# Keys of an attention kernel reversed in blocks of 128, and 3 of 16 half blocks of bias added by VectorE

## What is computed

```python
bias = tisa_bias(kernel_offsets, kernel_amplitudes, kernel_sharpness, l)   # depends on head and on i - j only
logits = jnp.einsum('bhld,bhmd->bhlm', q, k) * scale + bias[None]
attn = jax.nn.softmax(logits, axis=-1)
out = jnp.einsum('bhlm,bhmd->bhld', attn, v)
```

## Time and profile before

| | |
|---|---|
| median of 3 runs | 952.49 us (952.27 to 953.29) |
| the profiled execution | 943.6 us |
| its span, first to last instruction | 941.9 us |
| PE busy | 824.5 us, 88% |
| DVE busy | 707.9 us, 75% |
| ACT busy | 632.2 us, 67% |
| POOL busy | 244.0 us, 26% |
| granted TensorE clock, mean | 0.948 of full speed |

### The profile page before, as it was taken

How to read it: one execution, slowest core, us unless ns; L and a number is a source line. 1 busy time by engine, 2 the same in 40 slices (tenths; PEclk the granted TensorE clock), 3 DMA queues, 4 the chain that set the end, 5 groups by cost and what they waited for, 6 DMA issues and landing times.

```text
span 941.9 us, 22741 instructions
## 1 busy us (share of the span) xinstructions
PE 824.5 (88%) x9011; PEld 314.7 (33%) x9011; DVE 707.9 (75%) x1105; ACT 632.2 (67%) x1255; POOL 244.0 (26%) x543
## 2 busy tenths in 40 slices
PE   5189999999998999999998999999999999645770
PEld 2023333333333333333332223322232322245670
DVE  5388766777776887667789998899999898056545
ACT  6037767777775677767787988899889899501221
POOL 4010423200000414312300553331004001004773
PEclk9569999999999999999999999999999999866995
DMA  3655534654545454445313343232212220100123
GB/s 91 192 164 172 167 108 154 196 169 149 162 152 176 126 159 160 151 137 165 108 53 102 106 125 98 91 91 74 82 58 63 74 69 30 38 22 27 50 46 97
DMA packets 69439, 104.82 MB, mean 111 GB/s; under 512 B 15814, under 2 KB 45958, under 8 KB 69334
## 3 DMA queue, kind: packets, MB, share of 16 engines
q1 hardware_dynamic: 63254, 68.90, 25.2%
q10 hardware_dynamic: 4608, 31.46, 9.6%
q0 software_dynamic: 1472, 3.02, 1.3%
HBM read 84.23 MB, written 19.01 MB: 110 GB/s over the span
## 4 chain that ended last, share of the span: by engine, by line
PE 66%; DVE 10%; DMA 6%; SPq 5%; POOL 5%; ACT 4%; issue 4%; POOLq 0%; DVEq 0%
PE bank L1205 21%; PE bank L1224 16%; PE bank L1231 14%; PE bank L1185 8%; ACT prob_mem L844 4%; DVE unit_max L936 3%; PE bank L1158 2%; POOL moe_out L749 2%; DVE no_use L933 2%; PE bank L1267 2%; POOL prob_mem L738 2%; DMA prob_mem<-tokens,gather_u 1%; PE bank L1153 1%; DVE stats L882 1%; DMA prob_mem<-unit_sums 1%
## 5 line engine op out<-in xcount | busy, mean ns | idle before, releaser
L844 ACT ACTIVATE prob_mem<-bank 128x512 f32<-128x512 f32 x1024 | 555.8, 597 | 152.2 <-PE bank L1231 129.0
L933 DVE CUSTOM_DVE_ANT_0 no_use<-bank,w_moe 128x1024 bf16<-128x1024 f32 x256 | 311.9, 1223 | 111.4 <-PE bank L1185 110.7
L1185 PE MATMUL bank<-k_rows,q_rows 56*128 56x512 bf16 x1024 | 315.9, 392 | 25.2 <-DMA k_rows<-k_parts 17.3
L1224 PE MATMUL bank<-q_rows,k_rows 59*128 59x512 bf16 x1024 | 322.7, 385 | 4.6 <-DMA q_rows<-maxima_rows 0.9
L1205 PE MATMUL bank<-prob_mem,v_ring 128*32 128x256 f32 x4096 | 319.9, 386 | 6.0 <-issue 5.1
L936 DVE TENSOR_REDUCE unit_max<-bank 128x1 f32<-128x1024 f32 x256 | 297.9, 1216 | 21.5 <-PE bank L1185 19.9
L655 POOL CAST max_parts<-unit_max 128x8 bf16<-128x8 f32 x64 | 12.3, 191 | 574.6 <-DVE unit_max L933 327.4
L1231 PE MATMUL bank<-skew_mem,flip 96*32 96x512 bf16 x2048 | 159.5, 389 | 0.0
L1205 PEld LDWEIGHTS bank<-prob_mem,v_ring 128*32 128x32 f32 x4096 | 103.0, 110 | 159.8 <-ACT prob_mem L844 62.7
L1224 PEld LDWEIGHTS bank<-q_rows,k_rows 59*128 59x128 bf16 x1024 | 80.0, 93 | 218.3 <-issue 111.2
L1185 PEld LDWEIGHTS bank<-k_rows,q_rows 56*128 56x128 bf16 x1024 | 75.9, 93 | 36.0 <-issue 18.5
(11 more groups left out here) (164 smaller groups left out, 514.6 us busy)
## 6 DMA issues: line engine op xcount, KB each, us to landing
w_moe<-bias_rows ACTq DMA_DIRECT2D x32, 960.0 KB, 5.7
q_rows<-q_parts SPq DMA_DIRECT2D x256, 48.0 KB
k_rows<-k_parts SPq DMA_DIRECT2D x128, 96.0 KB
skew_mem<-bias_parts SPq DMA_DIRECT2D x32, 378.0 KB, 3.8
unit_sums<-o_ring SPq DMA_DIRECT2D x64, 128.0 KB, 2.6
w_moe<-in_L_ffn_w_dram SPq DMA_DIRECT2D x16, 256.0 KB, 3.1
q_parts<-prob_mem SPq DMA_DIRECT2D x8, 384.0 KB, 3.1
k_parts<-prob_mem SPq DMA_DIRECT2D x24, 128.0 KB, 2.6
```

The lines of the kernel that those rows point to most:

```text
L844: nc.scalar.activation(prob[:, kb, half * N:(half + 1) * N], b_bank(("exp", exp_no(n, kb, half))), ACT.Exp).then_inc(exp_done, 1)
L933: nc.vector.tensor_tensor_reduce(out=no_use[:, qb % 2, :], in0=scores, in1=bias, scale=1.0, scalar=LEAST, op0=ALU.add, op1=ALU.max, accum_ ...
L1185: return nc.tensor.matmul(sa_slot(QB * m + qb)[:, f, :], q_rows[rows, m % SLOTS, qb * P:(qb + 1) * P], k_rows[rows, m % SLOTS, f * N:(f + ...
L1224: return nc.tensor.matmul(b_bank(("exp", exp_no(n, kb, f))), k_rows[rows, n % SLOTS, kb * P:(kb + 1) * P], q_rows[rows, n % SLOTS, f * N:( ...
```

## The change

Half block `f=0` of blocks 1, 4 and 7 of each stage-1 unit gets its bias from DVE: an in-place addition on the PSUM bank of 512 values from the table, before the `block_max` of that block. PE leaves out the four bias matmuls of these half blocks (96 half blocks in all, 384 matmuls). So that one table serves both, with keys and with queries in the partitions, the keys are reversed within each block of 128; the table is then read forwards, in eight runs of 128, where it was read backwards before. Four tables are held where two were. SP waits for `exp_done` where it waited for `sb_done`.

```diff
+        def by_dve(n, kb, f):
+            return stage_of(n) == 0 and f == 0 and kb in (1, 4, 7)
...
-            queue.dma_start(bias_tab[:, n % 2, :], src).then_inc(tab_loaded[n % 2], 16)
+            queue.dma_start(bias_tab[:, n % 4, :], src).then_inc(tab_loaded[n % 4], 16)
...
+        def reversed_tiles(ap):
+
+            tiles_here = ap.shape[-1] // P
+            return bass.AP(ap.tensor, ap.offset + P - 1, [list(ap.ap[0]), [P, tiles_here], [-1, P]])
...
-                        sp.wait_ge(sb_done, 2 * QB * n)
+                        sp.wait_ge(exp_done, 2 * QB * n)
...
-                        act.wait_ge(sb_done, 2 * (QB * n + kb) + half + 1)
+                        i = exp_no(n, kb, half)
+                        if by_dve(n, kb, half):
+                            act.wait_ge(bias_added, dve_before[i + 1])
+                        else:
+                            act.wait_ge(sb_done, i + 1 - dve_before[i + 1])
...
-                nc.vector.tensor_copy(feat_b[:, gi * N:(gi + 1) * N], bank[:, gi, :]).then_inc(first_feat, 1)
+                nc.vector.tensor_copy(feat_b[:, gi * N:(gi + 1) * N], reversed_tiles(bank[:, gi, :])).then_inc(first_feat, 1)
...
-                    bias = bass.AP(tab.tensor, tab.offset, [list(tab.ap[0]), [-1, L]])
+                    bias = bass.AP(tab.tensor, tab.offset, [list(tab.ap[0]), [-P, QB], [1, P]])
...
+            def add_bias(n, kb):
+
+                half = b_bank(("exp", exp_no(n, kb, 0)))
+                at = L - P - kb * P
+                dve.wait_ge(raw_done, dve_before[exp_no(n, kb, 0) + 1])
+                nc.vector.tensor_tensor(half, half, bias_tab[:, n % 4, at:at + N], ALU.add).then_inc(bias_added, 1)
...
                 for kb in range(QB):
+                    if by_dve(n, kb, 0):
+                        add_bias(n, kb)
                     if n + 2 < NU:
                         block_max(n + 2, kb)
...
-                    nc.tensor.matmul(dst[:, 0:PW], weight, feat_b[:, c * PW:(c + 1) * PW], start=True, stop=True).then_inc(qk_mm, 1)
+                    piece = feat_b[:, c * PW:(c + 1) * PW]
+                    nc.tensor.matmul(dst[:, 0:PW], weight, piece if s else reversed_tiles(piece), start=True, stop=True).then_inc(qk_mm, 1)
...
+                        if by_dve(n, kb, f):
+                            ins.then_inc(raw_done, 1)
...
                         for f in range(2):
-                            bias_b(n, kb, f)
+                            if not by_dve(n, kb, f):
+                                bias_b(n, kb, f)
```

More of the change, by code:

```diff
@@ L91, in sandwich_kernel @@
         w_moe = sb("w_moe", [P, E, 2 * HID])
-        bias_tab = w_moe[:, 0:E // 2, :].rearrange("p e w -> p (e w)")[:, 0:2 * TAW].rearrange("p (s c) -> p s c", s=2)
+        bias_tab = w_moe[:, :, :].rearrange("p e w -> p (e w)")[:, 0:4 * TAW].rearrange("p (s c) -> p s c", s=4)
         skew_mem = sb("skew_mem", [P, 3 * L])
@@ L152, in sandwich_kernel @@
         rstd_twice = sb("rstd_twice", [P, TT])
-        flip = sb("flip", [96, 32], bf16)
+        pick = sb("pick", [96, 32], bf16)
         unit_max = sb("unit_max", [P, 2, QB])
@@ L208, in sandwich_kernel @@
         ones_ready = sem("ones_ready")
-        flip_ready = sem("flip_ready")
+        pick_ready = sem("pick_ready")
         sharp_ready = sem("sharp_ready")
@@ L238, in sandwich_kernel @@
         skew_loaded = [sem(f"skew_loaded{s}") for s in range(3)]
-        tab_loaded = [sem(f"tab_loaded{s}") for s in range(2)]
+        tab_loaded = [sem(f"tab_loaded{s}") for s in range(4)]
         sa_done = sem("sa_done")
@@ L242, in sandwich_kernel @@
         sb_done = sem("sb_done")
+        raw_done = sem("raw_done")
+        bias_added = sem("bias_added")
         exp_done = sem("exp_done")
@@ L366, in sandwich_kernel @@
         b_place = {what: i for i, what in enumerate(b_order)}
+        def by_dve(n, kb, f):
+            return stage_of(n) == 0 and f == 0 and kb in (1, 4, 7)
+        dve_before = [0]
+        for n in range(NU):
+            for kb in range(QB):
+                for f in range(2):
+                    dve_before.append(dve_before[-1] + by_dve(n, kb, f))
         def b_bank(what):
@@ L544, in _ @@
                     if n + LEAD >= SLOTS:
-                        sp.wait_ge(sb_done, 2 * QB * (n + LEAD - SLOTS + 1))
+                        sp.wait_ge(exp_done, 2 * QB * (n + LEAD - SLOTS + 1))
                     rows_of(n + LEAD)
@@ L624, in _ @@
             nc.gpsimd.memset(v_ring[:, :, :, DH:DH + 1], 1.0).then_inc(ones_ready, 1)
-            chain(nc.gpsimd.memset(flip[:], 0.0))
+            chain(nc.gpsimd.memset(pick[:], 0.0))
             for n in range(3):
-                chain(nc.gpsimd.affine_select(out=flip[:], in_=flip[:], compare_op=ALU.not_equal, fill=1.0,
-                                              base=-93 - n, pattern=[[3, 32]], channel_multiplier=1))
-            pool.sem_inc(flip_ready, 1)
+                chain(nc.gpsimd.affine_select(out=pick[:], in_=pick[:], compare_op=ALU.not_equal, fill=1.0,
+                                              base=-n, pattern=[[-3, 32]], channel_multiplier=1))
+            pool.sem_inc(pick_ready, 1)
             pool.wait_ge(bias_out, 1)
@@ L808, in turn_out @@
                 dst, src = feat_b[:, q * PW:(q + 1) * PW], b_bank(("turn", i))[:, 0:PW]
+                if t < 3:
+                    src = reversed_tiles(src)
                 if t in (0, 3):
@@ L929, in block_max @@
                     if qb == 0:
-                        dve.wait_ge(tab_loaded[m % 2], 16 * (m // 2 + 1))
-                    tab = bias_tab[:, m % 2, qb * P + L - 1:qb * P + L]
-                    bias = bass.AP(tab.tensor, tab.offset, [list(tab.ap[0]), [-1, L]])
-                    nc.vector.tensor_tensor_reduce(out=no_use[:, qb % 2, :], in0=scores, in1=bias, scale=1.0, scalar=LEAST, op0=ALU.add,
+                        dve.wait_ge(tab_loaded[m % 4], 16 * (m // 4 + 1))
+                    tab = bias_tab[:, m % 4, qb * P + L - P:qb * P + L - P + 1]
+                    bias = bass.AP(tab.tensor, tab.offset, [list(tab.ap[0]), [-P, QB], [1, P]])
+                    nc.vector.tensor_tensor_reduce(out=no_use[:, qb % 2, :].rearrange("p (k c) -> p k c", k=QB),
+                                                   in0=scores.rearrange("p (k c) -> p k c", k=QB), in1=bias, scale=1.0, scalar=LEAST, op0=ALU.add,
                                                    op1=ALU.max, accum_out=unit_max[:, m % 2, qb:qb + 1]).then_inc(max_done, 1)
@@ L1168, in _ @@
                 pe.wait_ge(first_feat, gi + 1)
-                nc.tensor.matmul(bank[:, 4 + 2 * gi, :], w_in_t[:, 2, :], feat_b[:, cols], start=True, stop=True).then_inc(first_q, 1)
+                nc.tensor.matmul(bank[:, 4 + 2 * gi, :], w_in_t[:, 2, :], reversed_tiles(feat_b[:, cols]), start=True, stop=True).then_inc(first_q, 1)
                 nc.tensor.matmul(bank[:, 5 + 2 * gi, :], w_in_t[:, 0, :], feat_b[:, cols], start=True, stop=True).then_inc(first_k, 1)
@@ L1225, in scores_b @@
                                         q_rows[rows, n % SLOTS, f * N:(f + 1) * N],
-                                        start=True, stop=(stage_of(n) == 1))
+                                        start=True, stop=(stage_of(n) == 1 or by_dve(n, kb, f)))
             def bias_b(n, kb, f):
                 for c in range(4):
-                    at = f * N - kb * P - 32 * c + L - 32
-                    ins = nc.tensor.matmul(b_bank(("exp", exp_no(n, kb, f)))[32 * c:32 * (c + 1), :], flip[:], skew[0:96, n % 3, at:at + N],
+                    at = f * N - kb * P + 32 * c + L - P
+                    ins = nc.tensor.matmul(b_bank(("exp", exp_no(n, kb, f)))[32 * c:32 * (c + 1), :], pick[:], skew[0:96, n % 3, at:at + N],
                                            start=False, stop=True, tile_position=(0, 32 * c))
@@ L1287, in _ @@
                     maxima_t(0, max_t(0))
-            pe.wait_ge(flip_ready, 1)
+            pe.wait_ge(pick_ready, 1)
             for n in range(NU):
```

## The result

The changed kernel takes 961.48 us in the median (958.84 to 963.61), against 952.4 for the kernel before: a ratio of 1.0092 (95% interval 1.0065 to 1.0119), so 8.8 us slower, 6 to 11. The forecast was 959.5, with 949 to 967 for 8 in 10.

What follows compares the result with a forecast made beforehand. PE was taken to bound stage 1. Plain additions 4.3, crowded 2.3 + 0.4, pieces 0.9, minus half a us in unit 0 gave about +7: 952.5 + 7 = 959.5 us, range 949 to 967 for 8 in 10.

Steps and rivals of the forecast that it cites:

- the ring: Reuse of PSUM banks in stage 1: PE's next second pair of score matmuls waits for an exponential; plain-block slack 0.10 us.
- rival A: The 1.81 us from first pair to next second pair holds: +4 to +10 us, 956 to 962.5; chance 0.60.
- the chain of 1.81: First score pair to next second pair, through addition and exponential: 0.43 + 0.69 + 0.03 + 0.60 + 0.06 = 1.81 us, before 1.75.
- D: No change: the 0.06 us loss is too small to read, only crowded blocks cost, 951 to 954 us; chance 0.11.
- PE's part: Bias matmuls PE gives up in stage 1: 96 half blocks of 0.22 us, at most 21 us.
- DVE free in time: In plain stage-1 blocks DVE is free 0.05 us before the addition is due, so the addition does not wait.
- Crowded blocks: Where statistics follow on DVE, additions start 0.25 us late at block 7, 0.57 at block 1: about 2.3 us more.
- Reversing, tables, SP's waits: Backwards reads, the forward-read table, table loads and SP's later waits in stage 1: taken as zero cost.
- Pieces between blocks: 18 additions with a piece behind them: eight at projections gain 0.08 us, ten lose some 0.15; together +0.9 us.
- rival B: The addition is dearer, by writing PSUM or DVE being late more often: 966 us at 0.76, 978 at 0.89; chance 0.16.
- Rival C: The addition hands over to ACT before its row ends, so faster: about 952 us, or 948; chance 0.13.
- the slow clock of unit 0: In unit 0 the slower clock makes bias matmuls dearer, so half a us was subtracted from the sum.

Runs made afterwards that it cites:

- the run with the order alone: The changed kernel with no DVE additions, PE adding all 16 half blocks; reversed keys, forward table and four tables kept: 952.22 us, ratio 0.9985.
- the run with the second half: The changed kernel with DVE adding the bias of half f=1 instead of f=0 at blocks 1, 4 and 7, in place: 946.37 us, ratio 0.9925.

## Why the prediction was right

**The bound and the ring.** The reading that PE bounds stage 1, and that an exponential just 0.10 early keeps the ring from binding, held. Taking the exponential out of the bank's loan, the time from the first pair to the bank's reuse, turned the loss into a gain with DVE's work unchanged. So rival A, the chain of 1.81, is what happened (961.48 within its 956 to 962.5). D, no change, is out with the interval and with the units of 12.76.

**The chain.** Forecast 1.81, measured 1.82. Links: to the addition 0.43 of 0.43, the addition 0.70 of 0.69, its handing over 0.03 of 0.03. The 0.06 of loss for each addition was 0.07 to 0.08; three of them make 0.22 where 0.18 was forecast.

**PE's part.** 0.22 a half block was forecast, 0.21 to 0.23 measured.

**DVE free in time.** Forecast in plain blocks; the addition started 0.43 after the pair at the places shown. Crowded blocks were forecast 0.25 and 0.57 late. The changed kernel, around the additions at blocks 7 and 1 in the interval of 13.56:

```profile
343.05 0.39 PE L1256 MATMUL bank<-q_rows,k_rows 59*128 59x512 bf16 x1
...
343.74 0.68 DVE L966 TENSOR_TENSOR bank<-bank,w_moe 128x512 f32<-128x512 f32 x1
...
346.41 0.39 PE L1256 MATMUL bank<-q_rows,k_rows 59*128 59x512 bf16 x1
...
347.40 0.68 DVE L966 TENSOR_TENSOR bank<-bank,w_moe 128x512 f32<-128x512 f32 x1
```

Counted from 0.43 after the pair they are 0.26 and 0.56 late, and the unit has 0.80 more than a plain one (0.82 forecast).

**Reversing, tables, SP's waits.** Forecast zero, measured zero by the run with the order alone.

**Pieces between blocks.** +0.9 us was forecast for 18 additions with a piece behind them, a gain of 0.08 at eight projections and a loss of 0.15 at the other ten, called shorter on PE. Around a projection, from first pair to next second pair, it was 2.38 (126.72 to 129.10) and is 2.30 (128.39 to 130.69), as forecast. Around a transpose it was 2.13 (112.13 to 114.26) and is 2.29 (110.06 to 112.35), near the 2.14 and 2.30 forecast. But four of the ten are projections to v, which take PE as long as the others. Before (L1158), then changed (L1190):

```profile
153.19 0.39 PE L1224 MATMUL bank<-q_rows,k_rows 59*128 59x512 bf16 x1
...
154.70 0.71 PE L1158 MATMUL bank<-w_in_t,prob_mem 128*128 128x128 f32 x4
...
155.58 0.38 PE L1224 MATMUL bank<-q_rows,k_rows 59*128 59x512 bf16 x1
```

```profile
154.80 0.39 PE L1256 MATMUL bank<-q_rows,k_rows 59*128 59x512 bf16 x1
...
157.10 0.39 PE L1256 MATMUL bank<-q_rows,k_rows 59*128 59x512 bf16 x1
```

It was 2.39 and is 2.30, so these four gain 0.09 each too, where a loss of 0.15 was counted. This step of the sum was wrong, and made it about 1 us too high.

**The dearer addition (rival B).** An addition that writes PSUM had no row. It is 0.698, against 0.692 in the median for the one that writes SBUF (first line of its view, ns min/median/max):

```profile
L974 DVE TENSOR_TENSOR summed<-bank,w_moe x96: 629/692/693, 59.7 to 476.0; 128x512 f32<-128x512 f32 x96
```

The 65 ns that the Trainium skill's page Perfetto Trace Analysis, Optimizing Scalar/DVE Operations, would put between PSUM and SBUF do not show between these two rows, which both read one operand from PSUM and differ in where they write; the measurement decides. Rival C, that ACT goes on before the row's end, is out too: 321.06 + 0.70 = 321.76, ACT at 321.79.

**The sum.** +7 was forecast. The intervals between copies give +6.8 in the 29 comparable units, the timed runs +8.8 with 6 to 11. The difference is not more than their uncertainty. That +6.8 lies so near to +7 is in part luck: the plain additions cost 0.07 to 0.08 instead of 0.06, about 1 us more in 72, and the pieces cost about 1 us less. The half us taken off for the slow clock of unit 0 cannot be read from any run: the first two intervals differ by -0.3 and +1.2, and the second of them is 13.65 instead of 12.71 in the trace of the order alone too.

**What the statement on the wait got roughly.** Some 20 us more of PE waiting for exponentials was forecast, 34 were measured. I counted 0.28 for each, by which the pair is late. The view counts the idle time between two weight loads, 0.41 in such a block:

```profile
322.44 0.09 PEld L1256 LDWEIGHTS bank<-q_rows,k_rows 59*128 59x128 bf16 x1 [0.41 <-ACT prob_mem L866]
```

The size forecast for that view was too small, and so was PE's busy share (92% for 96%), since both views measure something else than the delay of the pair; the length of the block was not touched by it.

## What to carry to other kernels

Work taken off the bounding engine is a gain only if its substitute fits into the slack of what it hands on. Here the pitch left 0.10 us between an exponential and the reuse of its bank, and the detour over a third engine put the exponential off by 0.17 (1.16 after the first pair instead of 0.99). The 0.22 saved on PE could not pay for that, since PE then waited for the bank. Even with no detour in that chain, the run with the second half, the bank let PE have only about 0.10 of the 0.22. Before moving such a piece, walk the chain from the producer to the reuse of the buffer; if it is longer than the new pitch, hand the data over in a buffer of its own, or choose the piece whose buffer is needed later.

## What was not expected of the hardware

The span of one profiled execution is a poor measure of a few us here. The kernel before was profiled at 941.9, and the version with the order alone, equal in the timed runs and in its plain units, at 952.9; so the 15.2 us between the spans of before and of the change are not its price. The same places differ from run to run: the three units that wait for the stored sums of a round to come back, 19.0, 13.5 and 12.8 us long in the one and 20.5, 14.9 and 14.5 in the other, 4.6 us more together; and the part after stage 2, 6.4 us longer. All the other executions profiled have longer waits in stage 2 than the one of before: from the 34th copy of the maxima to the last it takes 309 us there and 312 to 315 in the nine others. In the part after stage 2 of the changed kernel's trace ACT stands still for up to 6.4 us and DVE for up to 4.1. The waits put it down to "remote", which is another core or a queue that the profile does not know; 16.7 us of it stand on ACT in the version with the order alone, and the trace of before has no such line:

```profile
ACT prob_mem L890 <- remote: 26.2, 8, 6.4
```

What halts them the traces do not say, and it was not followed up.
